# A pre-norm transformer block on one core: weight parts made by GpSimd in the middle head groups, the last shared block behind the expert tiles, and the first group's orders on ScalarE, VectorE and TensorE

## The chip, the cores and the metric

The kernel runs on one core of one Trainium2 chip. The metric is the device time of one execution in microseconds (us). TensorE is called PE below, VectorE DVE, ScalarE ACT, GpSimd POOL, and SP is SyncE, the queue from which nearly all DMAs are issued.

## The reference, cut to what matters

One block over 2048 rows of width 256, in f32: attention with 16 query heads in 4 groups (4 key and value heads) of width 16, then a feed-forward part with 8 experts, two of them for each row, and a shared expert.

```
x = x + attn(layernorm(x))                    # T = 2048, D = 256
  q, k, v = x @ ternary(w_qkv).T              # q, k: RMS norm, rotary, q * gain
  y = softmax(causal(q k^T / 4)) v            # 4 groups of 4 heads share k and v
  attn = rms_norm(y) @ ternary(w_proj).T
x = x + ffn(layernorm(x))
  scores = sigmoid(x @ w_router); top 2 of 8, weights normalised
  ffn = sum_e combine[:, e] * (silu(x @ w1[e]) * (x @ w3[e])) @ w2[e]     # F = 176
      + (silu(x @ ws1) * (x @ ws3)) @ ws2                                 # FS = 352
```

## The kernel before, in words

**Numbers as two parts.** An f32 operand of a matmul is held as a high part (rounded to fp32r) and a low part (what is left), and products are sums over parts. So each feed-forward weight must be split once: a copy that rounds (high) and a subtraction (low). The weights go through in 19 `PIECES`: 2 of the shared expert's up weights, 1 of its down weights, 8 of the experts' up weights (128x704), 8 of their down weights (88x512).

**Stages.** (1) Layernorm, projection, rotary for the first group. (2) Attention, one head group `g` after another. A group is 40 units `u`, pairs of a 512-column block `j` of queries and a 128-row block `kt` of keys: for each, PE makes scores (`scores`, L1528) two units ahead, ACT takes the exponential (`exps`, L772), and PE multiplies by the values (`times_values`, L1548). The units on the diagonal, u = 0 to 3, 8 to 11, 20 to 23 and 36 to 39, are masked by POOL in between (`mask`, L608): the product of such a unit waits for its mask. (3) The shared expert over four 512-row blocks `j` in three slices each, 12 steps `n` of `up(n)` and `down(n)` (L1666, L1681, L1686), with the last attention and routing steps between. POOL sends the rows, sorted by expert, to DRAM (`send_rows`, L649). (4) 39 expert tiles of 128 rows (L1720, L1738), each result scattered to DRAM by POOL (L710). (5) The two expert results of each row are loaded (`yfin`, L525), added (L1423), and stored.

**What sets the order.** Each engine runs its own list, written out by hand, and waits on semaphores; nothing reorders it. Tables say after which unit PE does something besides: `FIRST_GROUP`, `MID_GROUP`, `LAST_GROUP`, and `AFTER` for stage 3. A "round" `(g, c)` turns 512 rows of q and k for group g (PE, L1489), DVE splits it (`take_round`: the high part L1036, the low part L1037, then `x_free`), and SP moves the three copies of each part into place (`move`, 9 DMAs of 64 KB; two more for the shifts with c = 0). Group g + 1's rounds are made in group g at u = 26 to 36. The first group's own rounds are made inside it, at u = 1, 8 and 16.

**SP's list before**: the moves of group 0; 3 DMAs that clear the buffer of sorted rows in DRAM (`clear_rows`, 1935 KB each); the moves for group 1; 6 more clears; the moves for group 2; 9 DMAs that write row numbers (`pad_ids`, 4-byte elements); the moves for the last group; and then, in the last group, the loads of the 19 pieces into a staging buffer with two places (L491 to L503), each waiting for the piece two before it. The high parts are cast by DVE (`high_piece`, L1128) up to piece 8 and by ACT (L825) behind, the low parts subtracted by POOL (`low_piece`, L615) and, for the last four, DVE (L1287). All of these stand between other work in the lists of the last group and stage 3.

Of the kernel before, what the change touches and what calls it, by code (L numbers as in the profile page):

```python
# [56 lines left out]
Q_PARTS, K_PARTS = (0, 1, 0), (0, 0, 1)  # L57
# [7 lines left out]
SHARED_PIECES, EARLY_PIECES, POOL_PIECES = KD + 1, 9, 15  # L65
PIECE_COLS = 3 * D
NST = 2
RES_AFTER = {4: 1, 7: 2, 8: 3}
# [8 lines left out]
    1: [("round", 0, 1)], 4: [("out", 0, 0)], 8: [("round", 0, 2)], 12: [("out", 0, 1)], 16: [("round", 0, 3)],  # L77
# [8 lines left out]
    30: [("step", 6, 1)], 31: [("step", 2, 2)], 32: [("step", 3, 2)], 34: [("step", 7, 1)], 37: [("step", 4, 2)],  # L86
# [57 lines left out]
def build(nc, x, w_qkv, w_proj, q_gain, w_router, w1, w2, w3, ws1, ws2, ws3, rope_cos, rope_sin, out):  # L144
# [3 lines left out]
    with ExitStack() as ctx:  # L148
# [90 lines left out]
        wk_c = sb("wk_c", [P, NT, HS, HD], F32, prep)  # L239
        part1 = sb("part1", [P, QKV * D // P], BF16, prep)  # L240
# [40 lines left out]
        ld_stage = [sem(f"ld_stage{i}") for i in range(NST)]  # L281
# [22 lines left out]
        ones_ready = sem("ones_ready")  # L304
        ld_qk = [sem(f"ld_qk{c}") for c in range(NC)]
# [9 lines left out]
        piece_hi = sem("piece_hi")  # L315
        piece_done = sem("piece_done")
# [18 lines left out]
        hid_lo_ready = sem("hid_lo_ready")  # L335
# [21 lines left out]
        rows_d = nc.dram_tensor("rows_by_expert", (ROWS, ROW), F32, kind="Internal").ap()  # L357
        pair_d = nc.dram_tensor("pair_out", (2 * T + ROWS, D), F32, kind="Internal").ap()
# [28 lines left out]
        def piece_parts(n):  # L387

            buf = stage[:, n % NST, :]
            kind, *at = PIECES[n]  # L390
            if kind == "shared":
                k, = at
                return [(buf[:, 0:2 * FS].rearrange("p (w f) -> p w f", w=2), ws_hi[:, k], ws_lo[:, k])]
            if kind == "shared down":
                spans = [(P, 0, SH - 1), (shared_rows(SH - 1), SH - 1, SH)]
                return [(buf[0:r, a * D:b * D].rearrange("p (m d) -> p m d", d=D), ws2_hi[0:r, a:b, :],
                         ws2_lo[0:r, a:b, :]) for r, a, b in spans]
            if kind == "up":
                w, k, half = at
                es, fs = slice(half * E // 2, (half + 1) * E // 2), slice(w * F, (w + 1) * F)  # L400
                return [(buf[:, 0:E // 2 * F].rearrange("p (e f) -> p e f", f=F), w13_hi[:, k, es, fs],
                         w13_lo[:, k, es, fs])]
            h, pair = at
            es = slice(2 * pair, 2 * pair + 2)
            return [(buf[0:FH, 0:2 * D].rearrange("p (e d) -> p e d", d=D), w2_parts[0:FH, h, es, 0, :], w2_parts[0:FH, h, es, 1, :])]

        loads_of = {"shared": 2, "shared down": SH, "up": 1, "down": 1}

        def staged(n):

            return 16 * sum(loads_of[p[0]] for p in PIECES[n % NST:n + 1:NST])

# [4 lines left out]
        def _(sp):  # L417
# [19 lines left out]
            def move(g, c):  # L437
# [3 lines left out]
                sp.wait_ge(x_free, round_use(g, c))  # L441
                cs = slice(c * CH, (c + 1) * CH)
                for hf in range(2):
                    for n, part in enumerate(Q_PARTS):
                        sp.dma_start(qk_f[n:P:4, (g + 1) % 2, hf, cs],  # L445
                                     qT_f[2 * HD * hf:2 * HD * (hf + 1), part, cs]).then_inc(ld_qk[c], 16)
                if g > 0 or c >= K_BY_ACT:
                    move_k(sp, g, c, ld_qk[c])
# [7 lines left out]

# [11 lines left out]
            for c in range(NC):  # L468
                move(2, c)
# [1336 lines left out]
```

## Time and profile before

| | us |
|---|---|
| three runs | 583.75, 587.46, 588.2 (median 587.46) |
| the profiled execution | 586.47, its span 584.7, mean granted TensorE clock 0.91 |
| busy: PE, ACT, DVE, POOL | 474.4, 362.2, 314.9, 171.1 |

The span is shorter than the execution by 1.8 us, which lie around the first and last instruction. Busy time is read against the span; matmuls overlap, so a PE that is busy all the time may still wait a little in each unit. The granted clock is a share of 2.4 GHz. A wait is put down to the semaphore that came last.

### The profile page before, as it was taken

What the parts mean: (1) busy time and instruction counts of PE and PEld (TensorE: products, weight loads), DVE (VectorE), ACT (ScalarE), POOL (GpSimd) and SP (SyncE); (2) the same over time, 40 slices, a digit from 0 to 9 for tenths busy, and PEclk for the clock granted to TensorE, in tenths of its full rate; (3) what the DMA queues carried; (4) which work ended last, traced back from release to release, by engine and by line L of the source; (5) the groups of instructions that cost most, each with busy time, mean ns of one, the idle gap of its engine ahead of it and who ended that gap; (6) DMA issues with size and microseconds to landing.
All of it is one profiled execution on the core that took longest, in us unless ns stands there. A gap on an engine that the chain in (4) does not pass through costs nothing.

```text
span 584.7 us, 9812 instructions
## 1 busy us (share of the span) xinstructions
PE 474.4 (81%) x3202; PEld 265.1 (45%) x3202; DVE 314.9 (54%) x886; ACT 362.2 (62%) x567; POOL 171.1 (29%) x222
## 2 busy tenths in 40 slices
PE   1693949898999999999398978848888789999930
PEld 1581313333333333333143523326767679888930
DVE  6963615843732148031266485445948657666626
ACT  4244839897999999999359566615252335555520
POOL 3711100002110111103242145045455814444430
PEclk9878869999999999999789888868988989999975
DMA  7111011974799649624421113211111424444349
GB/s 207 36 42 41 2 40 30 278 204 107 214 298 296 164 77 4 2 53 110 138 57 62 26 46 114 62 34 64 30 55 40 123 73 119 117 119 128 101 132 353
DMA packets 77526, 61.37 MB, mean 105 GB/s; under 512 B 26984, under 2 KB 70600, under 8 KB 77480
## 3 DMA queue, kind: packets, MB, share of 16 engines
q1 hardware_dynamic: 73784, 51.04, 37.5%
q0 software_dynamic: 3408, 9.34, 4.4%
q8 instruction: 27, 0.44, 0.3%
q10 hardware_dynamic: 288, 0.39, 0.3%
q14 instruction: 19, 0.16, 0.1%
HBM read 19.88 MB, written 29.34 MB: 84 GB/s over the span
## 4 chain that ended last, share of the span: by engine, by line
PE 44%; DVE 15%; issue 13%; SPq 8%; DMA 7%; ACT 6%; POOL 5%; another core or an unknown queue 1%; ACTq 0%; POOLq 0%; DVEq 0%
PE ps L1548 14%; PE ps L1528 10%; PE ps L1720 6%; ACT prob L772 5%; SPq L445 4%; PE ps L1738 3%; POOL rows_by_expert L649 2%; PE ps L1468 2%; SPq L366 2%; PE ps L1557 1%; DMA qk<-qT 1%; PE ps L1711 1%; DMA yfin<-pair_out 1%; PE ps L1742 1%; PE ps L1489 1%
## 5 line engine op out<-in xcount | busy, mean ns | idle before, releaser
L772 ACT ACTIVATE prob<-ps 128x1024 f32<-128x1024 f32 (+3 forms) x320 | 260.1, 922 | 76.1 <-PE ps L1528 69.1
L1548 PE MATMUL ps<-prob,v_sb 128*32 128x512 f32 (+3 forms) x1280 | 156.8, 564 | 17.8 <-DVE o_sb L1048 9.0
L1528 PE MATMUL ps<-qk 64*128 64x512 f32 (+3 forms) x640 | 122.5, 448 | 24.1 <-DMA qk<-qT 15.3
L608 POOL TENSOR_SCALAR_AFFINE_SELECT prob<-prob 128x512 f32<-128x512 f32 x64 | 41.6, 652 | 233.7 <-ACT prob L772 232.8
L1528 PEld LDWEIGHTS ps<-qk 64*128 64x128 f32 x640 | 54.5, 194 | 118.2 <-ACT prob L772 82.2
L1548 PEld LDWEIGHTS ps<-prob,v_sb 128*32 128x32 f32 x1280 | 25.9, 110 | 65.1 <-issue 34.7
L710 POOL DMA_INDIRECT pair_out<-yo,xg x39 | 37.5, 963 | 56.1 <-DVE yo L1404 55.8
L1048 DVE COPY o_sb<-ps 128x512 f32<-128x512 f32 x16 | 11.0, 690 | 67.7 <-PE ps L1548 67.2
L1666 PE MATMUL ps<-x2T,ws_hi 128*128 128x512 f32 (+1 forms) x96 | 33.0, 428 | 5.4 <-DVE hid L1273 5.4
L649 POOL DMA_INDIRECT rows_by_expert<-xs,slots x32 | 31.2, 976 | 14.2 <-issue 8.6
L1036 DVE CAST qT<-ps 96x512 fp32r<-96x512 f32 x16 | 11.0, 686 | 38.6 <-PE ps L1489 38.6
L1738 PE MATMUL ps<-w_parts,ht_hi 88*128 x78 | 27.8, 437 | 1.4 <-issue 1.2
L856 ACT ACTIVATE sil<-ps 128x176 f32<-128x176 f32 x39 | 12.4, 318 | 25.5 <-PE ps L1720 25.5
L1391 DVE SCALAR_TENSOR_TENSOR hid<-sil,xg,ps 128x176 f32<-128x176 f32 x39 | 15.5, 397 | 18.1 <-ACT sil L856 17.6
L867 ACT COPY yl<-ps 128x256 f32<-128x256 f32 x39 | 14.5, 373 | 14.6 <-PE ps L1742 9.9
L1404 DVE TENSOR_TENSOR yo<-ps,yl 128x256 f32<-128x256 f32 x39 | 16.6, 425 | 11.6 <-ACT yl L867 10.6
L678 POOL TENSOR_TENSOR hid_lo<-hid,hid_hi 128x512 fp32r<-128x512 f32 (+1 forms) x12 | 15.5, 1299 | 24.5 <-ACT hid_hi L819 24.4
L1666 PEld LDWEIGHTS ps<-x2T,ws_hi 128*128 128x128 f32 (+1 forms) x96 | 17.6, 193 | 10.8 <-DVE hid L1273 6.3
L1054 DVE RECIPROCAL rec<-ps 128x16 f32<-128x16 f32 x16 | 4.1, 258 | 33.7 <-PE ps L1557 33.6
L615 POOL TENSOR_TENSOR w_lo<-stage,w_hi 128x704 fp32r<-128x704 f32 x8 | 13.5, 1692 | 28.6 <-DVE w_hi L1128 28.6
L1720 PE MATMUL ps<-w_hi,xt_hi 128*128 x78 | 19.9, 338 | 0.7 <-DVE xt_lo L1385 0.6
L1666 PE MATMUL ps<-x2T,ws_lo 128*128 128x512 f32 (+1 forms) x48 | 20.4, 426 | 0.0
(203 smaller groups left out, 781.2 us busy)
## 6 DMA issues: line engine op xcount, KB each, us to landing
rows_by_expert<-pads SPq DMA_DIRECT2D x9, 1935.0 KB, 20.4
qk<-qT SPq DMA_DIRECT2D x138, 64.0 KB, 2.1
xg<-rows_by_expert SPq DMA_DIRECT2D x39, 129.0 KB
yfin<-pair_out SPq DMA_DIRECT2D x8, 512.0 KB, 7.1
stage<-in_w SPq DMA_DIRECT2D x8, 352.0 KB
x_sb<-in_x SPq DMA_DIRECT2D x4, 512.0 KB, 6.8
qk<-shT SPq DMA_DIRECT2D x8, 256.0 KB, 4.8
res<-in_x SPq DMA_DIRECT2D x4, 512.0 KB, 4.1
```

The lines of the kernel that those rows point to most:

```text
L445: sp.dma_start(qk_f[n:P:4, (g + 1) % 2, hf, cs], qT_f[2 * HD * hf:2 * HD * (hf + 1), part, cs]).then_inc(ld_qk[c], 16)
L608: nc.gpsimd.affine_select(out=t, in_=t, compare_op=ALU.is_ge, fill=0.0, base=0, pattern=[[0, HPG], [1, P]], channel_multiplier=-1).then_in ...
L649: nc.gpsimd.indirect_dma_start(out=rows_d, out_offset=bass.IndirectOffsetOnAxis(ap=slots[:, j % 2, w, t:t + 1], axis=0), in_=xs_of[j][:, w ...
L678: nc.gpsimd.tensor_tensor(hid_lo[0:r, n % 2, :], hid[0:r, n % 2, :], hid_hi[0:r, n % 2, :].bitcast(F32), ALU.subtract).then_inc(hid_lo_rea ...
L710: nc.gpsimd.indirect_dma_start(out=pair_d, out_offset=bass.IndirectOffsetOnAxis(ap=xg[:, i % NXG, ID:ID + 1].bitcast(I32), axis=0), in_=yo ...
L772: nc.scalar.activation(prob[:, u % NPB, 2 * hf:2 * hf + 2, c0:CH], ps[:, b:b + 2, c0:CH], ACT.Exp, scale=SCALE).then_inc(exp_done, 1)
L1404: V.tensor_tensor(yo[:, i % NYO, :], ps[:, 4 + i % 2, 0:D], yl[:, i % 2, :], ALU.add).then_inc(yo_ready, 1)
L1528: ins = M(ps[:, 2 * (n % NSB) + h, c0:CH], qk[rows, par, PAIRS, kt * P:(kt + 1) * P], qk[rows, par, hf, j * CH + c0:(j + 1) * CH], start=T ...
L1548: ins = M(ps[VW * h:VW * (h + 1), O_BANK, c0:CH], v_sb[:, kt, :], prob[:, u % NPB, h, c0:CH], start=(kt == 0), stop=(u == LAST_OF[j]), ski ...
L1666: ins = M(ps[0:r, 2 * w + n % 2, :], wt[:, k, w, m * P:m * P + r], a[j][:, k, :], start=(i == 0), stop=(i == 3 * KD - 1))
L1720: ins = M(ps[:, i % 2, 0:UP], a[:, i % 2, k, :], w[:, k, bass.ds(e, 1), :].rearrange("p e f -> p (e f)"), start=(n == 0), stop=(n == 3 * K ...
L1738: M(ps[:, 4 + i % 2, :], ht_hi[0:FH, i % 2, h, :], w2_parts[0:FH, h, bass.ds(e, 1), :, :].rearrange("p e c d -> p (e c d)"), start=(h == 0 ...
```

## The change: what it does

Eight edits, together.

1. **The pieces are split two groups earlier, by POOL alone, and through DRAM.** SP loads a raw piece into one of `NRAW` = 3 places (`load_raw`), POOL casts and subtracts it (`split_piece`), SP stores both parts to new DRAM tensors (`store_parts`), of which two pieces fit at a time (`NSPLIT` = 2). POOL does 1 piece behind the mask of u = 3, 3 behind u = 11 and 6 behind u = 23 in groups 1 and 2 (`SPLIT_AT`). In the last group SP loads the finished parts: `ws`, `ws2`, `w13` (2 DMAs), and `w2_parts` after the attention.
2. **SP's list**: 4 clears ahead of the moves for group 1, 3 behind, then the first raw loads, 2 clears, and the pieces between the moves for group 2 and for the last group. The 9 writes of row numbers stand between the pieces of group 2.
3. All piece work leaves DVE, ACT and POOL in the last group and stage 3.
4. In `take_round` DVE signals the high part by itself (`hi_taken`); SP and ACT issue the moves of high parts at once and those of low parts after `x_free`.
5. First group: the round of c = 1 moves from u = 1 to u = 0; ACT's moves for it from before unit 3 to before unit 4; DVE's norm is cut into squares and scaling, and the squares stand earlier.
6. Stage 3: steps 4 to 7 of block 3 stand earlier in `AFTER`; step (4, 2) moves from u = 37 to 39; POOL keeps the low hidden part of n = 0 to 3, DVE takes it from n = 4; the rows of blocks 2 and 3 are sent without anything in between; `choose`, `place` and `list_tiles` stand earlier on DVE.
7. `up(11)` and `down(9)` to `down(11)` go behind the 39 tiles.
8. DVE adds the results of blocks 0 and 1, then the last shared block, then blocks 2 and 3. `yfin` lies over `w13` instead of `x2T`.

```diff
-Q_PARTS, K_PARTS = (0, 1, 0), (0, 0, 1)
+Q_PARTS, K_PARTS = (HI, LO, HI), (HI, HI, LO)
-NST = 2
+NRAW, NSPLIT = 3, 2
 FIRST_GROUP = {
-    1: [("round", 0, 1)], 4: [("out", 0, 0)], ...
+    0: [("round", 0, 1)], 4: [("out", 0, 0)], ...
-    ... 34: [("step", 7, 1)], 37: [("step", 4, 2)],
+    ... 34: [("step", 7, 1)], 39: [("step", 4, 2)],
-LOW_PIECES = {3: range(0, 3), 11: range(3, 5), 23: range(5, EARLY_PIECES)}
+SPLIT_AT = {3: 1, 11: 3, 23: 6}
+LOW_ON_DVE = range(4, FLAT)
 def move(g, c):                                   # SP
-    sp.wait_ge(x_free, round_use(g, c))
+    for want, ready, at in ((HI, hi_taken, NC * g + c + 1), (LO, x_free, round_use(g, c))):
+        sp.wait_ge(ready, at)
...
+def load_raw(n):
+    if n >= NRAW:
+        sp.wait_ge(split_done, n - NRAW + 1)
+    for r, at, shape, src, _ in pieces_of(n):
+        sp.dma_start(... raw[0:r, n % NRAW, ...], src).then_inc(ld_raw[n % NRAW], 16)
+def store_parts(n):
+    sp.wait_ge(split_done, n + 1)
+    ... sp.dma_start(to[part], ... parts_f[0:r, n % NSPLIT, part, ...]).then_inc(st_parts[n % NSPLIT], 16)
+def next_piece(n):
+    if n + NRAW - 1 < len(PIECES):
+        load_raw(n + NRAW - 1)
+    store_parts(n)
-clear_rows(0, 3)
+clear_rows(0, 4)
 for c in range(NC):
     move(1, c)
-sp.wait_ge(s_ready, 2 * NU)
-clear_rows(3, blocks)
+clear_rows(4, 7)
+sp.wait_ge(s_ready, 2 * NU + 2 * (LAG + 1))
+for n in range(NRAW - 1):
+    load_raw(n)
+clear_rows(7, blocks)
+for n in range(4):
+    next_piece(n)
 for c in range(NC):
     move(2, c)
+    if c < NC - 1:
+        next_piece(4 + 2 * c)
+        next_piece(5 + 2 * c)
+for n in range(10, 14):
+    next_piece(n)
+    number_pads(n - 10)
 for c in range(NC):
     move(3, c)
+    for n in range(14 + 2 * c, min(16 + 2 * c, len(PIECES))):
+        next_piece(n)
+        number_pads(n - 10)
...
+def split_piece(n):                               # POOL
+    pool.wait_ge(ld_raw[n % NRAW], raw_loaded(n))
+    if n >= NSPLIT:
+        pool.wait_ge(st_parts[n % NSPLIT], parts_stored(n - NSPLIT))
+    for r, at, shape, _, _ in pieces_of(n):
+        nc.gpsimd.tensor_copy(hi, a).then_inc(split_step, 1)
+        pool.wait_ge(split_step, taken["n"])
+        ins = nc.gpsimd.tensor_tensor(lo, a, hi.bitcast(F32), ALU.subtract)
+    ins.then_inc(split_done, 1)
+for g in range(NKV - 1):
     for u in range(NU):
         if on_diagonal(u):
             mask(g, u)
+        for _ in range(SPLIT_AT.get(u, 0) if g > 0 else 0):
+            split_piece(n)
...
+if n == FLAT - 1:                                 # PE, up(n)
+    pe.wait_ge(hid2_ready, TILES)
+    pe.wait_ge(ht_lo_ready, TILES)
+if n == FLAT_FIRST:                               # PE, down(n)
+    pe.wait_ge(yo_ready, TILES)
...
+up(FLAT - 1)                                      # PE, behind the tiles
+for n in range(FLAT_FIRST, FLAT):
+    down(n)
```

**POOL, from the masks of the middle groups on.** `prob` is the tile that a mask cuts, `raw` a loaded piece, `parts` its two parts. Before, the groups 0 to 2 are one loop of 16 masks, and the first piece stands behind the first four masks of the last group:

```order
76 L608 AFFINE_SELECT prob<-prob 128x4x128
77 L618 REGISTER_ALU
78 L618 COMPARE_AND_BRANCH
79 L608 AFFINE_SELECT prob<-prob 128x4x128 x4
80 L615 TENSOR_TENSOR ws_lo<-stage,ws_hi 128x704 x2
```

With the change, the loop is written out; row 46 is the 16 masks of group 0 and the first 4 of group 1:

```order
46 L667 AFFINE_SELECT prob<-prob 128x4x128 [waits exp_done] x20
47 L678 CAST parts<-raw 128x352 [waits ld_raw0]
48 L681 TENSOR_TENSOR parts<-raw,parts 128x352 [waits split_step]
49 L678 CAST parts<-raw 128x352
50 L681 TENSOR_TENSOR parts<-raw,parts 128x352 [waits split_step]
51 L667 AFFINE_SELECT prob<-prob 128x4x128 [waits exp_done] x4
52 L678 CAST parts<-raw 128x352 [waits ld_raw1]
```

The masks of u = 8 to 11 of group 1 (row 51) now stand behind a cast that waits for a load.

**SP, around the clears.** L445 and L366 move `qT` (DVE's parts of q and k) into `qk`. Before:

```order
21 L366 DMA qk<-qT 32x512 x3
22 L445 DMA qk<-qT 32x512 x6
23 L366 DMA qk<-qT 32x512 x3
24 L454 DMA rows_by_expert<-pads 128x15x258 x6
25 L445 DMA qk<-qT 32x512 x6
```

With the change (L379 and L387 move `qT`, L494 loads a raw piece, L502 stores parts):

```order
34 L379 DMA qk<-qT 32x512 x2
35 L387 DMA qk<-qT 32x512
36 L486 DMA rows_by_expert<-pads 128x15x258 x3
37 L494 DMA raw<-in_ws 128x352 x4
38 L486 DMA rows_by_expert<-pads 128x15x258 x2
39 L494 DMA raw<-in_ws 128x256 x2
40 L494 DMA raw<-in_ws 96x256
41 L502 DMA ws_parts<-parts 128x352 x4
```

The first raw loads stand behind all moves for group 1 and behind three clears.

## Rows read from the trace of the kernel before

**Rows 1.** Stages: us busy (instructions) of each engine, granted clock, DMA share, GB/s.

```profile
...
137.10:206.00 68.90, 67.13 (x517) 22.96 (x514) 26.34 (x58) 64.50 (x81) 10.27 (x16) 1.00 0.82 222
...
274.70:392.90 118.20, 89.76 (x622) 38.28 (x622) 61.85 (x240) 69.03 (x91) 37.09 (x41) 0.84 0.23 68
392.90:473.00 80.10, 66.57 (x378) 55.02 (x374) 54.86 (x138) 31.57 (x50) 46.15 (x42) 0.94 0.20 64
...
561.00:585.00 24.00, 0.17 (x2) 0.00 (x0) 10.26 (x10) 0.37 (x1) 1.93 (x2) 0.52 0.82 279
...
```

**Rows 2.** PE's waits: line, releaser, us in total, times, longest.

```profile
...
PE ps L1528 <- DMA qk<-qT: 15.3, 3, 7.5
...
PE ps L1548 <- DVE o_sb L1048: 9.0, 1, 9.0
PE ps L1548 <- POOL prob L608: 8.5, 1, 8.5
...
PE ps L1686 <- POOL hid_lo L678: 3.1, 2, 1.8
...
```

**Rows 3.** POOL in time, first masks of three quarters: start, us, what, idle before.

```profile
...
150.88 0.64 POOL L608 TENSOR_SCALAR_AFFINE_SELECT prob<-prob 128x512 f32<-128x512 f32 x1 [9.94 <-ACT prob L772]
...
200.23 0.64 POOL L608 TENSOR_SCALAR_AFFINE_SELECT prob<-prob 128x512 f32<-128x512 f32 x1 [24.98 <-ACT prob L772]
...
269.03 0.64 POOL L608 TENSOR_SCALAR_AFFINE_SELECT prob<-prob 128x512 f32<-128x512 f32 x1 [24.90 <-ACT prob L772]
...
```

**Rows 4.** DVE in time: high part of the round (2, 0).

```profile
...
184.22 0.69 DVE L1036 CAST qT<-ps 96x512 fp32r<-96x512 f32 x1 [3.04 <-PE ps L1489]
...
```

**Rows 5.** SP's issues in time: start, us, line, what, how many.

```profile
...
102.87 8.49 SPq L454 DMA_DIRECT2D rows_by_expert<-pads  x3
...
150.74 30.19 SPq L454 DMA_DIRECT2D rows_by_expert<-pads  x6
...
214.09 22.27 SPq L472 DMA_DIRECT2D rows_by_expert<-pad_ids  x9
254.53 3.67 SPq L445 DMA_DIRECT2D qk<-qT  x6
...
261.51 6.54 SPq L445 DMA_DIRECT2D qk<-qT  x6
...
```

**Rows 6.** DMA rate while six clears are under way (columns of Rows 1).

```profile
...
150.70:185.60 34.90, 33.93 (x262) 11.16 (x254) 15.03 (x34) 33.19 (x43) 5.18 (x8) 1.00 1.07 292
...
```

**Rows 7.** DMA issues from 185 to 187 us: KB each, us to landing.

```profile
...
qk<-qT SPq DMA_DIRECT2D x1, 64.0 KB, 6.8
```

**Rows 8.** Chain of waits from 280 to 292 us: start, us, what.

```profile
...
285.61 3.31 DMA stage<-in_ws
...
```

**Rows 9.** POOL's groups by form: busy us, mean ns, idle before, releaser.

```profile
...
L615 POOL TENSOR_TENSOR w_lo<-stage,w_hi 128x704 fp32r<-128x704 f32 x8 | 13.5, 1692 | 28.6 <-DVE w_hi L1128 28.6
...
L635 POOL COPY xs<-xs 128x1024 f32<-128x1024 f32 x2 | 2.1, 1050 | 8.9 <-DVE xs L1191 8.9
...
```

**Rows 10.** First PE work after the wait for o_sb (columns of Rows 1).

```profile
...
290.00:296.00 6.00, 4.65 (x24) 1.62 (x24) 2.89 (x10) 0.90 (x1) 2.10 (x3) 0.53 0.45 120
...
```

**Rows 11.** DVE and PE in time around the second long stall.

```profile
...
383.63 1.38 DVE L1191 TENSOR_SCALAR xs<-y_sb,mv,sm 128x256 f32<-128x256 f32 x4
...
391.55 0.66 PE L1562 MATMUL ps<-ident,xs 128*128 128x128 f32 x4
...
```

**Rows 12.** PE in time from the last shared block to the tiles.

```profile
...
461.37 0.62 PE L1666 MATMUL ps<-x2T,ws_hi 128*96 128x512 f32 x2
...
464.15 0.28 PE L1681 MATMUL ps<-ws_hi,hid_hi 128*128 128x256 f32 x1
...
471.65 0.93 PE L1711 MATMUL ps<-ident,xg 128*128 128x128 f32 x4 [0.94 <-DMA xg<-rows_by_expert]
...
```

**Rows 13.** DVE in time: a step beside a POOL subtraction; a block taken.

```profile
...
408.67 1.63 DVE L911 SCALAR_TENSOR_TENSOR sm<-sm 128x4 f32<-128x4 f32 x1
...
427.74 1.22 DVE L1279 TENSOR_TENSOR y_sb<-ps,y_sb 128x1024 f32<-128x1024 f32 x1
...
```

More of the change, by code:

```diff
@@ L239, in build @@
         wk_c = sb("wk_c", [P, NT, HS, HD], F32, prep)
+        split = ExitStack()
+        raw = sb("raw", [P, NRAW, PIECE_COLS], F32, split)
+        parts = sb("parts", [P, NSPLIT, 2, PIECE_COLS], F32R, split)
+        split.close()
         part1 = sb("part1", [P, QKV * D // P], BF16, prep)
@@ L280, in build @@
         ld_small = sem("ld_small")
-        ld_stage = [sem(f"ld_stage{i}") for i in range(NST)]
+        ld_raw = [sem(f"ld_raw{i}") for i in range(NRAW)]
+        split_done = sem("split_done")
+        split_step = sem("split_step")
+        st_parts = [sem(f"st_parts{i}") for i in range(NSPLIT)]
+        ld_ws = sem("ld_ws")
+        ld_w13 = sem("ld_w13")
+        ld_w2 = sem("ld_w2")
         ld_res = sem("ld_res")
@@ new lines, in _ @@
+            sp.dma_start(ws[:].bitcast(F32), ws_d).then_inc(ld_ws, 16)
+            sp.dma_start(ws2[:].bitcast(F32)[:, :, 0:SH - 1], ws2_d[:, :, 0:SH - 1]).then_inc(ld_ws, 16)
+            last_rows = shared_rows(SH - 1)
+            sp.dma_start(ws2[0:last_rows].bitcast(F32)[:, :, SH - 1], ws2_d[0:last_rows, :, SH - 1]).then_inc(ld_ws, 16)
+            sp.wait_ge(x_free, step_use(3, 0))
+            sp.dma_start(res[:], x_t[:, TPC:2 * TPC, :]).then_inc(ld_res, 16)
+            for part in range(2):
+                sp.dma_start(w13[:, part].bitcast(F32), w13_d[:, part]).then_inc(ld_w13, 16)
@@ L511, in _ @@
+            for j in range(2, NC):
+                sp.wait_ge(x_free, step_use(3, j - 1))
+                sp.dma_start(res[:], x_t[:, j * TPC:(j + 1) * TPC, :]).then_inc(ld_res, 16)
+            sp.wait_ge(pv_done, NPB + NU * NKV)
+            sp.dma_start(w2_parts[0:FH].bitcast(F32), w2_d).then_inc(ld_w2, 16)
             sp.wait_ge(rows_ready, 1)
@@ L1418, in _, with finish @@
                     tile_out(i - 2)
-            for c in range(NC):
+            def finish(c):
                 dve.wait_ge(ld_fin[c], 32)
@@ L1697, in _ @@
             pe.wait_ge(exp_done, NSB + 2 * NU * NKV)
-            pe.wait_ge(piece_done, SHARED_PIECES)
-            for n in range(FLAT + 2):
-                if n < FLAT:
-                    up(n)
+            pe.wait_ge(ld_ws, 48)
+            for n in range(FLAT - 1):
+                up(n)
                 after((n, 0))
```

354 lines of the change are left out of this document (171 added, 183 removed).

## The prediction, made before the change was run

> **What bounds the kernel now.** I read the stages first, then PE's waits, then the other engines in time where PE waits. In a middle group PE is busy 67.13 of 68.90 us at full clock, ACT 64.50, while DVE has 26.34 and POOL 10.27 [rows 1]: attention is bound by PE, and POOL looks free. The last group takes 118.20 us with PE at 89.76 and the granted clock at 0.84; the shared stage 80.10 with PE 66.57, DVE 54.86 and POOL 46.15. PE's longest waits there are one of 9.0 us for DVE's `o_sb` and one of 8.5 for a POOL mask [rows 2]. In both groups POOL's idle time is long but in pieces: it ends with the masks, which come in fours at fixed times (u = 8 of group 1 after 9.94 us of idleness, u = 36 after 24.98 and, in group 2, 24.90) [rows 3]. A list is worked off in order, so the question is whether the pieces put before a mask are done when that mask is wanted. If not, PE stops, since it has no slack there.
>
> **The first group.** DVE's signal for the high part saves the low half's time ahead of the first moves (0.7 us, the length of the high cast [rows 4]) in three rounds, and the earlier c = 1 and the cut norm some 1.2 to 1.3 in two of them; these waits are part of the 15.3 us behind `qT`'s moves [rows 2]. I take 2.0 + 1.2 + 0.7 = 3.9, less 1 because a fourth clear now lies before group 1's moves: **-3** (0 to -4).
>
> **Stall 1, group 1, u = 8.** The mask of u = 8 stands behind piece 0. It was wanted at 150.9 [rows 3], now at 147.9. SP used to begin the clears at 150.74; now, 3 us and one cast's 0.7 earlier, at about 147. Three clears take SP 8.49 us to issue [rows 5], so the raw loads go out at 155.5. The clears' data then move at 292 GB/s [rows 6], and 1935 KB is 6.6 us, three 19.8. If the loads queue behind them, they start at about 168; a small move issued while the last clear was draining landed only after 6.8 us [rows 7]. A free load takes 3.31 [rows 8]; with 2.5 for this smaller one and 3 for the four operations of piece 0 (a subtraction twice as wide is 1.69, a copy of 1024 columns 1.05 [rows 9]) the mask comes at about 174: **+26**. If the loads don't queue it is 155.5 + 3.3 + 3 = 162 and +14; with full clears and a landing of 6.8, +30. I take 26, since rows 7 show a transfer held on that very queue. Of "DMA: Bandwidth & Descriptors" in the Trainium skill, the section on queues, rings and completion order says that each DMA engine takes one queue's descriptors in ring order; by that rule it is the 26, without it the 14. The held move agrees.
>
> **Stall 2, group 1, u = 36.** Six pieces (4 to 9) stand between u = 23 and this mask, and SP's list threads them through the moves of the rounds. Before, the high part of round (2, 0) was made at 184.9 [rows 4] and the mask was wanted 15.3 us later [rows 3]. SP needs 6.98 for the moves of a first round and 0.61 for an issue [rows 5]. Piece 9's load goes out behind the moves of c = 0, four issues or so per piece and the moves of c = 1: 6.98 + 2 x 1.8 + 5.6 + 1.8 + 0.6 = 18.5. Its landing (3.3) and split (2.4 to 2.7) end at 24.5 to 25.5: **+10**. Low end 7, if small issues take less than 0.61; high end 14, with a landing of 6.8.
>
> **Stall 3, group 2, u = 36.** The same with pieces up to 18: the load of piece 18 goes out at 18 to 19, its places come free when the parts of piece 16 are stored (1.2 and 3.3 more), its split adds 2: 25 where 15.25 is there: **+10**. But writes of row numbers stand between, and each took SP 2.5 us (22.27 for nine [rows 5]) against the 0.6 I count; so 6 to 16.
>
> **The clock.** After the wait for `o_sb` PE works at a clock of 0.53 for 4.65 busy us [rows 10], so a stall costs some 2 more: **+6** for three (3 to 7).
>
> **The last group.** DVE's casts and the loads before them are gone, so the 9.0 for `o_sb` [rows 2] go with 2 of clock: **-11** (-7 to -12). The second, 8.5 for a mask that stood behind pieces on POOL, doesn't go whole. Step (4, 2) follows it, and needs `scale_x2`, which DVE ended at 385.0; PE came to that step's transposes at 391.55 [rows 11]. It can now be there at about 386.5, with 1 of clock: **-6** (-3 to -10). Fewer DVE and POOL operations otherwise: **-2** (0 to -4).
>
> **The shared stage.** `up(11)` took PE 2.8 us (461.37 to 464.15), the three `down` 7.5 with 2.7 of waits, so 4.8 [rows 12]. Together some 7.5 leave the way to the tiles. The 3.1 for `hid_lo` [rows 2] go with it. DVE's routing steps are freed of POOL's subtractions beside them (one of 4 columns took 1.63 instead of the 0.16 of its like [rows 13]) and stand earlier: 3. **-13.5** (-7 to -18). The Trainium skill, in "SBUF — State Buffer" on who interferes with whom, says that VectorE and GpSimd share a port pair with an exclusive lock; the row of 1.63 agrees. By that rule the 38 casts and subtractions now slow DVE in the middle groups instead. DVE is busy 26.34 of 68.90 there [rows 1], which covers it unless it falls on a round.
>
> **The tail.** What went behind the tiles is PE's work in 24 us in which it has 0.17 and DMAs move 279 GB/s [rows 1]. Only DVE's addition of one more block, 1.22 us [rows 13], may show: **+1.3** (0 to +3).
>
> **The sum** is made against the profiled execution, 586.5: -3 + 26 + 10 + 10 + 6 - 11 - 6 - 2 - 13.5 + 1.3 = +17.8, so 604.3. The profiled execution is 1.0 below the median of the three runs (587.46), so **605**. With all the terms at their best it is 569, with all at their worst 636; these don't fall together, and 592 to 618 is the forecast's own range.
>
> **The rivals.**
>
> *The waits are short and the gains win nothing (0.20).* The loads don't queue behind the clears, and the other two stalls sit at their low ends: 14 + 7 + 6 with 5 of clock is 32, against 34.2 of net gains (the other terms): 584.3, with the median's 1.0 some 585, and 577 to 592 with the gains' bounds. For it: no row shows a load from DRAM behind a clear, only the small move. Against it: that move's 6.8 us.
>
> *The pieces fit into POOL's idle time (0.07), the other side.* The mechanism is piece work that is ready each time before the next mask. It decides at u = 8 of group 1: the raw piece must have landed by about 145, which is before SP's clears end by every row of SP here, unless clears issued into an empty queue cost SP almost nothing. Then the stalls and their clock fall away and the gains stay: 586.5 - 34.2 + 1.0 = **553**. It turns into slower once the stalls with their clock come to over 34 us.
>
> *The stalls are longer than summed (0.13).* In group 2 the nine writes of row numbers take SP 22.27 us wherever they stand, and the small transfers queued behind them land in 6.8 instead of 3.3. Then stall 3 is at 16 and stall 2 at 14, stall 1 at 30 with 1 more of clock: 605 + 4 + 4 + 6 + 1 = **620**, up to 636.
>
> *The change doesn't do what it says:* SP's list, written out, has the loads where the diff says, behind three clears, and POOL's masks of u = 8 behind piece 0. I give this nothing of its own.
>
> **How the numbers follow.** The forecast has 0.60. A change of 1% (581.6 and 593.3) is what a measurement here can tell. Faster: 0.07, and 0.08 of the first rival: 0.15. Within 1%: the other 0.12 of it and 0.02 of the forecast's low edge: 0.14. Slower: 0.71. The range that holds 8 in 10 takes in most of the first rival and half of the third: 580 to 622.
>
> **What would show it.** Three waits of PE for POOL's `prob`, about 26 us in 148 to 174, 10 in group 1 and 10 in group 2, each before a mask that started late because a cast on POOL waited for `raw`; group 1 at some 105 us instead of 68.9, the last group at 100 instead of 118, the shared stage near 67, the tail still near 25, with no DVE wait of 9.0. If POOL's casts find their pieces landed, or SP's clears take less than 3 us in all, I am wrong at once; if the stalls are there but the time isn't, the gains of the last two stages were larger than their rows. A group 2 without a stall would say that the writes of row numbers cost SP little.

## The result, and the profile after

| | before | changed |
|---|---|---|
| executions, us | 583.75, 587.46, 588.2, 588.58 | 622.69, 630.32, 632.83, 635.2 |
| median | 587.83 | 631.58 |
| profiled execution, its span | 586.47, 584.7 | 622.69, 620.9 |
| mean granted clock | 0.91 | 0.891 |

The change makes the kernel slower: ratio 1.0652, 95% interval 1.0587 to 1.0716. Executions that were disturbed are in no ratio: here 632.83 and 635.2 (at a clock of 0.875), later 619.0 in experiment 1, 1393.16 and 577.75 in experiment 6, and one of 670.41 of the kernel before. The profiled execution was the shortest of its four. 605 was forecast, with 580 to 622 as the range: the direction is right, the size is not.

The stages of the changed kernel, cut at the same places as in [rows 1] (columns: us of the stretch, busy us and instructions of each engine, granted clock, DMA share, GB/s). They are group 1, group 2, the last group, the shared stage and the tail:

```profile
...
134.20:250.90 116.70, 72.65 (x522) 24.31 (x518) 25.03 (x58) 64.42 (x81) 36.73 (x44) 0.78 0.77 216
250.90:341.30 90.40, 70.95 (x514) 23.63 (x514) 28.36 (x57) 64.71 (x81) 28.21 (x35) 0.89 0.41 82
341.30:437.30 96.00, 83.27 (x618) 35.51 (x618) 54.79 (x222) 68.47 (x90) 21.53 (x31) 0.95 0.35 126
437.30:509.80 72.50, 60.05 (x330) 49.96 (x330) 47.99 (x149) 25.11 (x39) 28.18 (x28) 0.91 0.34 93
...
596.30:620.90 24.60, 7.28 (x50) 6.26 (x48) 12.71 (x13) 1.59 (x3) 1.97 (x3) 0.74 0.79 272
...
```

Group 1 takes 116.7 us with PE busy 72.65, where it took 68.9 with 67.13. PE's waits over the whole execution (us in total, times, longest):

```profile
...
PE ps L1609 <- POOL prob L667: 57.9, 4, 25.9
PE ps L1589 <- DMA qk<-qT: 11.7, 3, 6.9
...
PE ps L1747 <- DVE y_sb L1346: 4.4, 2, 2.5
...
PE ps L1609 <- DVE o_sb L1113: 3.4, 2, 2.6
...
```

The wait for POOL's `prob` was 8.5 us once [rows 2]; now it is 57.9 in four, 57.6 of it in groups 1 and 2. A ledger from mark to mark in the two profiled executions (the marks are the first mask of a group, the mask of u = 39 of the last group, the first tile's transposes, the end of the span):

| stretch | before | changed | difference | forecast |
|---|---|---|---|---|
| to the first mask of group 1 | 137.1 | 134.2 | -2.9 | -3 |
| groups 1 and 2 | 137.6 | 207.1 | +69.5 | +52 |
| last group, to the mask of u = 39 | 116.3 | 94.2 | -22.1 | -19 |
| on to the first tile | 80.6 | 73.0 | -7.6 | -13.5 |
| tiles and tail | 113.0 | 112.4 | -0.6 | +1.3 |
| sum | 584.7 | 620.9 | +36.2 | +17.8 |

**Stall 1.** The chain of waits of the changed kernel around u = 8 of group 1 (start, us, what):

```profile
...
148.00 1.94 SPq L486
...
149.98 6.85 SPq L486
...
156.88 6.02 SPq L494
...
162.94 9.26 DMA raw<-in_ws
...
172.81 0.93 POOL parts L681
...
```

It runs as forecast: SP issues three clears, then the raw loads from 156.88 on, which itself takes it 6 us, and they land 9.26 us later; POOL's piece 0 ends before 175.1, where the mask starts. PE waited 25.9 us (26 were forecast).

**Stalls 2 and 3.** SP's queue in the changed kernel (start, us of issuing, line, what, how many; L379 and L387 are moves, L494 a raw load, L502 stores of parts):

```profile
...
147.38 9.46 SPq L486 DMA_DIRECT2D rows_by_expert<-pads  x3
156.88 8.49 SPq L494 DMA_DIRECT2D raw<-in_ws  x4
...
210.98 2.39 SPq L379 DMA_DIRECT2D qk<-qT  x4
...
217.97 1.91 SPq L494 DMA_DIRECT2D raw<-in_w  x1
219.92 1.98 SPq L502 DMA_DIRECT2D w_parts<-parts  x2
...
233.05 0.79 SPq L494 DMA_DIRECT2D raw<-in_w  x1
233.88 1.83 SPq L502 DMA_DIRECT2D w_parts<-parts  x2
...
```

From 198.9 to 210.98 SP does nothing: it waits for the round (2, 0). Behind that move stand the loads of pieces 6 and 7 and the stores of pieces 4 and 5. POOL in the same execution (start, us, what, idle before and what ended it):

```profile
...
134.21 0.64 POOL L667 TENSOR_SCALAR_AFFINE_SELECT prob<-prob 128x512 f32<-128x512 f32 x1 [4.63 <-ACT prob L825]
...
172.25 0.48 POOL L678 CAST parts<-raw 128x352 fp32r<-128x352 f32 x1 [33.22 <-DMA raw<-in_ws]
...
226.49 0.77 POOL L678 CAST parts<-raw 128x704 fp32r<-128x704 f32 x1 [20.25 <-DMA w_parts<-parts]
...
240.84 0.77 POOL L678 CAST parts<-raw 128x704 fp32r<-128x704 f32 x1 [0.78 <-DMA w_parts<-parts]
...
243.31 1.81 POOL L667 TENSOR_SCALAR_AFFINE_SELECT prob<-prob 128x512 f32<-128x512 f32 x3
...
268.53 0.61 POOL L678 CAST parts<-raw 88x512 fp32r<-88x512 f32 x1
269.23 1.28 POOL L681 TENSOR_TENSOR parts<-raw,parts 88x512 fp32r<-88x512 f32 x1
270.45 0.61 POOL L678 CAST parts<-raw 88x512 fp32r<-88x512 f32 x1
271.14 2.12 POOL L681 TENSOR_TENSOR parts<-raw,parts 88x512 fp32r<-88x512 f32 x1
...
```

Piece 6's cast starts at 226.49 after 20.25 us of idleness, piece 9's at 240.84, and only at 243.31 comes the mask of u = 36, which had 16.80 us of PE waiting behind it. The row of 172.25 is stall 1: POOL idle for 33.22 us, for a raw load.

**The clock after a stall** (columns as in the stages):

```profile
...
150.00:175.00 25.00, 0.00 (x0) 0.00 (x0) 3.33 (x10) 1.18 (x3) 2.59 (x4) 0.58 1.08 295
175.00:181.00 6.00, 5.19 (x28) 1.53 (x32) 0.00 (x0) 1.02 (x3) 3.75 (x7) 0.50 1.12 277
181.00:187.00 6.00, 5.59 (x48) 1.93 (x48) 1.87 (x7) 6.00 (x7) 1.54 (x3) 0.98 1.08 292
...
```

In the 6 us behind stall 1 PE was busy 5.19 at half the clock (1.2 GHz), so 2.6 us are lost there. In groups 1 and 2 PE is busy 9.7 us longer than before with the same work, behind four stalls (the fourth is below).

**The tail.** From the timeline, PE and DVE behind the tiles:

```profile
...
596.34 2.94 PE L1730 MATMUL ps<-x2T,ws 128*96 128x512 f32 x12
...
602.94 0.64 PE L1752 MATMUL ps<-ws,hid_lo 96*128 96x256 f32 x4
606.28 2.48 DVE L1475 TENSOR_TENSOR y_sb<-y_sb,yfin 128x1024 f32<-128x1024 f32 x2 [4.14 <-DMA yfin<-pair_out]
...
```

The shared work moved there is over at 603.6, before the first result of an expert lands for DVE at 606.28.

### The profile page after: what moved, and what is told of

It is laid out like the page before. It is cut to its first block, busy times and chain, and to the rows that moved or that the text cites. A ratio compares the mean times of both kernels' runs of the same rounds, so it can differ in the third digit from the quotient of the medians.

```text
span 620.9 us, 9852 instructions
## 1 busy us (share of the span) xinstructions
PE 476.0 (77%) x3202; PEld 263.3 (42%) x3202; DVE 303.0 (49%) x880; ACT 356.4 (57%) x557; POOL 182.6 (29%) x244
## 4 chain that ended last, share of the span: by engine, by line
PE 45%; DVE 19%; SPq 14%; issue 8%; DMA 7%; ACT 5%; POOL 1%; DVEq 0%; ACTq 0%; POOLq 0%
PE ps L1609 13%; PE ps L1589 8%; PE ps L1785 6%; SPq L379 6%; ACT prob L825 4%; PE ps L1804 3%; PE ps L1730 3%; SPq L494 2%; SPq L387 2%; PE ps L1529 2%; SPq L486 2%; PE ps L1645 1%; DMA raw<-in_ws 1%; PE ps L1618 1%; SPq L502 1%
## 5 line engine op out<-in xcount | busy, mean ns | idle before, releaser
L1609 PE MATMUL ps<-prob,v_sb 128*32 128x512 f32 (+3 forms) x1280 | 162.0, 581 | 61.3 <-POOL prob L667 57.9
L1113 DVE COPY o_sb<-ps 128x512 f32<-128x512 f32 x16 | 11.1, 691 | 134.3 <-PE ps L1609 133.9
L678 POOL CAST parts<-raw 128x704 fp32r<-128x704 f32 (+4 forms) x23 | 14.9, 649 | 98.7 <-DMA raw<-in_ws 33.2
L1730 PE MATMUL ps<-x2T,ws 128*128 128x512 f32 (+1 forms) x144 | 40.4, 434 | 0.9 <-DVE hid L1332 0.9
L1785 PE MATMUL ps<-w,xt_hi 128*128 x156 | 31.7, 325 | 1.7 <-DVE xt_lo L1436 1.7
L1730 PEld LDWEIGHTS ps<-x2T,ws 128*128 128x128 f32 (+1 forms) x144 | 28.1, 201 | 8.8 <-DVE hid L1332 1.4
L681 POOL TENSOR_TENSOR parts<-raw,parts 128x704 fp32r<-128x704 f32 (+4 forms) x23 | 30.7, 1334 | 1.9
L882 ACT ACTIVATE sil<-ps 128x512 f32<-128x512 f32 (+1 forms) x12 | 7.2, 596 | 32.5 <-PE ps L1730 25.4
L1785 PEld LDWEIGHTS ps<-w,xt_hi 128*128 128x128 f32 x156 | 24.5, 188 | 2.1 <-issue 2.1
L916 ACT COPY yl<-ps 128x256 f32<-128x256 f32 x39 | 14.5, 373 | 14.7 <-PE ps L1808 9.6
```

Of the source, the lines that this page charges most:

```text
L681: ins = nc.gpsimd.tensor_tensor(lo, a, hi.bitcast(F32), ALU.subtract)
L1609: ins = M(ps[VW * h:VW * (h + 1), O_BANK, c0:CH], v_sb[:, kt, :], prob[:, u % NPB, h, c0:CH], start=(kt == 0), stop=(u == LAST_OF[j]), ski ...
L1730: ins = M(ps[0:r, 2 * w + n % 2, :], wt[:, k, w, m * P:m * P + r], a[j][:, k, :], start=(i == 0), stop=(i == 3 * KD - 1))
L1785: ins = M(ps[:, i % 2, 0:UP], a[:, i % 2, k, :], w[:, k, bass.ds(e, 1), :].rearrange("p e f -> p (e f)"), start=(n == 0), stop=(n == 3 * K ...
```

## The experiments

All on one core. Every ratio is to runs of the kernel before on the same chip; absolute times come from different chips (the medians of the kernel before lie between 582.55 and 588.25), so small differences are read from the ratios. Waits and stretches are those of one profiled execution each. "Wait for POOL" is PE's wait for `prob`.

**1. The raw loads ahead of the clears.**

```diff
+sp.wait_ge(s_ready, ...); load_raw(0); load_raw(1)
 clear_rows(4, 7)
-sp.wait_ge(s_ready, ...); load_raw(0); load_raw(1)
+next_piece(0); next_piece(1)
 clear_rows(7, 9)
```

> The changed kernel with the raw loads of pieces 0 and 1 ahead of the three clears (the last two clears behind the stores of piece 1). Theory 'the first stall is the queue': a transfer on SP's queue moves behind what was issued before it. The loads go out at 147.4, land at about 152, piece 0 takes 2.8: PE's wait for POOL before the product of u = 8 falls from 25.9 us to 3 to 7, the waits of 16.8 and 15.0 stay, and the time falls by 20 to 24, to 600 in the profiled execution (changed kernel: 622.7). Rival 'POOL or the DMA engines are slow there whatever the order': the wait stays over 15 and the time over 612.

612.9 us, ratio 1.040 (1.032 to 1.048). The first wait fell from 25.9 to 2.9 us; the others were 22.7 in two (5 of them new, at u = 20 of group 1) and 15.2. The order of SP's list made stall 1. The time fell less than the 20 to 24: from a ratio of 1.065 to 1.040, some 15 us, and PE's waits for masks by 16.8 us in all. The profiled execution took 619.0, where 600 was expected.

**2. Piece 0 loaded from ScalarE's queue, the clears in front as they were.**

```diff
 exps(1, 8)                                      # ACT
+nc.scalar.dma_start(raw piece 0)                # two loads
-load_raw(0)                                     # SP, behind the clears
```

> The changed kernel with the four raw loads of piece 0 issued by ScalarE behind the exponentials of unit 8 of group 1 (about 149.5 us), while the three clears stay ahead on SP's queue and are being moved. Theory 'each queue is in order, and queues share the engines': the loads land 3 to 8 us after their issue, the wait falls from 25.9 us to 8 to 12, the time by 13 to 18. Rival 'the DMA engines work off everything in order of issue': the wait stays at 22 to 26 and the time within 5 of the changed kernel's.

(Piece 0 has two loads; the four that the text speaks of are those of pieces 0 and 1.) The clears on SP, the two loads on ScalarE's queue and POOL's first cast, in time:

```profile
...
148.31 9.73 SPq L486 DMA_DIRECT2D rows_by_expert<-pads  x3
...
148.53 1.19 ACTq L862 DMA_DIRECT2D raw<-in_ws  x2
...
155.95 0.48 POOL L678 CAST parts<-raw 128x352 fp32r<-128x352 f32 x1 [15.23 <-DMA raw<-in_ws]
...
```

The loads were issued 0.2 us after the first clear and POOL could cast 7.4 us after that. Only two of the three clears had been issued by then, so the short time alone would not tell a second queue from a shorter one. The trace does: the first clear landed 9.9 us after its issue, at about 158, and the second at about 164, both behind the loads. From 149 to 155 us SP's queue moved 1.56 MB of the clears and ScalarE's the 0.36 MB of the loads, side by side: a second queue overtakes. The wait fell to 7.9. So the theory of queues stands, but the time did not fall as expected (626.6 us, ratio 1.0675, 1.061 to 1.074): waits later in groups 1 and 2 rose from 31.8 to 44.1 us. The load of piece 1 was still behind the clears on SP's queue (issued from 158.08, cast at 171.37), and a new wait of 11.9 stood at u = 20.

**3. No pieces at all, with the shared block behind and ahead of the tiles.**

```diff
-load_raw(n + 2); store_parts(n)                 # SP
+both parts of piece n copied from the input, DRAM to DRAM
-split_piece(n)                                  # POOL
```

> The changed kernel without raw loads and without POOL's casts and subtractions: at the same places of SP's list the inputs are copied from DRAM to DRAM into both parts (so the low parts are wrong, and the bytes written stay about the same). Theory 'the three stalls are POOL's list': all three waits for masks are gone, groups 1 and 2 take 138 to 140 us together instead of 207, and the time is 550 to 556, that is 0.94 of the kernel before. Rival 'the piece transfers themselves hold up the rounds of q and k': waits of PE for the moves of qT appear in place of the masks' and the time stays over 565.

> As no_pieces, but with up(11) and down(9) to down(11) ahead of the 39 tiles again, as in the kernel before. Theory 'the work behind the tiles is hidden by the last transfers': 6 to 9 us slower than no_pieces, all of it before the first tile. Rival 'it is only moved': within 2 us of no_pieces, the stretch behind the last tile being shorter by as much as the stretch before the tiles is longer.

573.5 us (0.973, 0.967 to 0.979) and 577.2 (0.982, 0.976 to 0.988). Groups 1 and 2 took 139.5 us as expected. But the time missed the 550 to 556, because the last group took 110.5, not 94: PE waited 10.4 us for DVE, which waited for the residual's rows. That wait was new. From the mask of u = 39 to the end it was 186.2 and 192.4 us, 6.2 more with the shared block ahead. The whole difference is smaller than the 6 to 9 expected: the medians are 3.7 apart, and the last group of the second run was 3.1 us shorter, which that edit does not explain.

**4. All transfers, but POOL doesn't wait for them or work on them.**

```diff
-pool.wait_ge(ld_raw...); pool.wait_ge(st_parts...); cast; subtract
+pool.sem_inc(split_done, 1)                     # parts filled once with a constant
```

> The changed kernel with all its transfers, but POOL neither waits for them nor casts nor subtracts: it fills the parts once with a constant and only counts the pieces (so all feed-forward weights are that constant; the earlier no_pieces had an artefact of its own, a wait of 10.4 us for a residual load). Theory 'the whole loss is POOL's list holding masks back': groups 1 and 2 take 138 to 141 us together, the last group 93 to 96, the time 554 to 560. Rival 'transfers': over 565, with waits for moves of qT.

577.6 us, ratio 0.983 (0.978 to 0.988): neither theory. The waits for masks are gone, but two others stand among PE's waits:

```profile
...
PE ps L1587 <- DMA qk<-qT: 16.4, 5, 6.9
...
PE ps L1643 <- DVE y_sb L1234: 9.2, 1, 9.2
...
```

L1587 waits for moves of `qT` (16.4 in five; 4.0 of it in groups 1 and 2, with 1.2 more for a shift, 1.0 in the last group, and the rest in the first), and L1643 waits 9.2 us for DVE's residual. Groups 1 and 2 take 146.3 us instead of 139.5 and the last group 106.8 instead of 94. So without the stalls, and with this list of SP's, SP's queue is the next bound, about 7 us in the middle groups, and the residual's load another 9. In the changed kernel neither wait shows: there the stalls gave the queue time.

**5. Pieces ahead of the moves, and a third place for parts.** The first changes SP's order only:

```diff
-for n in range(4): next_piece(n)
+for n in range(6): next_piece(n)
 for c in range(4):
     move(2, c)
-    next_piece(4 + 2 * c), next_piece(5 + 2 * c)      # c < 3
+    next_piece(6 + 2 * c), next_piece(7 + 2 * c)      # c < 2; group 2 alike
```

> The changed kernel with the stores and loads that follow pieces 4 and 5 (14 and 15 in group 2) ahead of the moves of round (2, 0) ((3, 0)) in SP's list; the later pairs move up with them. Theory 'the second and third stall are SP's order': there SP waited idle from 198.9 to 211.0 us for a round while piece 6's load and piece 4's store stood behind it. The waits of 16.8 and 15.0 us fall to 0 to 6 each, the 25.9 stays, and the time falls by 22 to 34, profiled execution 589 to 600 (changed kernel: 622.7). Rival 'bytes and places': the 1056 KB that a piece loads and stores at about 290 GB/s and the wait for a place of parts set the pace, and both waits stay over 11.

600.4 us, ratio 1.021 (1.017 to 1.026). What is left of the wait for POOL from 182 us on:

```profile
...
PE ps L1609 <- POOL prob L667: 6.9, 2, 5.9
...
```

16.8 became 5.9 and 15.0 became 1.0, both as expected; the first wait was 23.1. The other gives POOL more room:

```diff
-NRAW, NSPLIT = 3, 2
+NRAW, NSPLIT = 3, 3
```

> The changed kernel with three places for finished parts instead of two, nothing else. Theory 'SP's order': piece 6's raw load is behind the moves of round (2, 0) whatever the places, so the waits of 16.8 and 15.0 fall by 1 to 5 each and the 25.9 not at all; time 3 to 9 less. Rival 'the round trip of the stores': POOL's casts waited 27 and 31 us in all for stores of parts, so with a third place the two waits fall to under 8 each, and the time by over 16.

622.9 us, ratio 1.058 (1.051 to 1.065): the waits were 23.4, 15.1 and 13.4 (25.9, 16.8 and 15.0 before), 5.8 less in all, where two executions of the changed kernel differ by 3.9 (experiment 7). Order decided it, not places or bytes.

**6. Three rearrangements that keep all the work.** The first:

```diff
-SPLIT_AT = {3: 1, 11: 3, 23: 6}
+SPLIT_AT = {3: 2, 11: 4, 23: 4}
 move(1, 0); move(1, 1)
+load_raw(0); load_raw(1)
 move(1, 2); move(1, 3)
-...
+clears one at a time behind pieces 1 and 3, three in group 2
+one piece behind the moves of each round
+number_pads(0 to 8) in a row behind the moves for the last group
```

> The changed kernel with all its work, in another order: the first two raw loads ahead of the moves of rounds (1, 2) and (1, 3), POOL's pieces 2, 4 and 4 behind the units 3, 11 and 23 instead of 1, 3 and 6, one clear at a time between the pieces and three clears in group 2, and one piece behind the moves of each round. By my reading (order alone made the stalls) the waits for masks are under 4 us each, groups 1 and 2 take 139 to 147 us instead of 207, and the time is 555 to 565, 0.95 to 0.96 of the kernel before. Rival 'there is no room on the DMA queue': clears, pieces and moves of group 1 come to over 60 us of transfer in 69, and a wait of 8 to 15 us is left: 568 to 580.

604.8 us, ratio 1.029 (1.021 to 1.036), outside both. The waits for POOL came down to 3.2, 11.1 and 0.9, but a wait of 19.2 us for DVE stood in the last group. DVE's row of the residual, and SP's rows before it:

```profile
...
338.25 0.88 DVE L1244 SCALAR_TENSOR_TENSOR y_sb<-ps,y_scale,res 128x256 f32<-128x256 f32 x2 [20.72 <-DMA res<-in_x]
...
```

```profile
...
309.44 18.63 SPq L512 DMA_DIRECT2D rows_by_expert<-pad_ids  x9
328.19 2.50 SPq L560 DMA_DIRECT2D res<-in_x  x1
...
```

The nine writes of row numbers, 7.5 KB each, took SP 18.63 us in a row, and the residual's load stood behind them. The second takes up both waits: the stores and loads behind pieces 4 to 7 ahead of the move of round (2, 0), the writes spread over group 2, and two clears between the rounds of group 0.

> The rearranged kernel, with its two remaining waits taken up: 2, 3 and 5 pieces in group 1 and 2, 4 and 3 in group 2, the stores behind pieces 4 to 7 ahead of the moves of round (2, 0), five clears in group 0 (two of them before the move of its last round), one in the middle of group 1, three in group 2, and the nine writes of row numbers spread over group 2 instead of in a row in front of the residual's load. In the rearranged kernel these were waits of 11.1 us for a mask and of 19.2 us for DVE's residual, whose load stood behind 18.6 us of such writes. Theory 'each wait is a place in SP's list': both are under 4 us, groups 1 and 2 take 139 to 147 us, the last group 93 to 99, the time is 556 to 572. Rival 'SP's queue has no room for all of it': the waits come back elsewhere (moves of qT, masks) with over 10 us in all, and the time is over 575.

572.6 us, ratio 0.982 (0.977 to 0.986): just outside the 556 to 572. The residual's wait was 2.9, all but one of the masks' waits under 1.3, and that one 14.3, in group 2, behind two clears; groups 1 and 2 took 155.8 us, not 139 to 147. The third moves those as well:

```diff
 move(0, 1)
+clear_rows(0, 1)
 move(0, 2)
-clear_rows(0, 2)
+clear_rows(1, 3)
 move(0, 3)
-clear_rows(2, 5)
+clear_rows(3, 6)
 ...                                             # one more in group 1
-clear_rows(6, 8)                                # ahead of piece 12's load
+SPLIT_AT of group 2: {3: 2, 11: 3, 23: 4}
```

> The second rearrangement with the clears spread once more: six in group 0 (one behind the moves of its second round, two behind the third, three behind the fourth), two in group 1, one in group 2 behind piece 11, and 2, 3 and 4 pieces in group 2. In the run before, two clears in front of the raw load of piece 12 left one wait of 14.3 us for the mask of u = 20 of group 2. If a wait is only what stands ahead in the queue, no wait for a mask is over 3 us, groups 1 and 2 take 139 to 143 us, and the time falls by 13 to 19, to 554 to 560 (0.95 to 0.96 of the kernel before). If the queue has no room left, 5 us or more of waiting come back at another mask or at the moves of qT, and the time is over 563.

> The same with up(11) and down(9) to down(11) ahead of the tiles. By the pair no_pieces and no_pieces_shared_first (573.5 and 577.2, the stretch from the mask of u = 39 to the end 6.2 us longer) this is 4 to 7 us slower than rearranged_3. If that difference was chance, they are within 2 us.

**563.5 us, ratio 0.968 (0.966 to 0.971)**: faster than both kernels, though above the 554 to 560. Its waits that are left, and its groups 1 and 2 and last group:

```profile
...
PE ps L1624 <- POOL prob L682: 7.4, 3, 6.0
...
PE ps L1660 <- DVE y_sb L1251: 3.1, 1, 3.1
...
```

```profile
...
131.90:279.60 147.70, 136.00 (x1028) 46.12 (x1026) 55.34 (x114) 128.94 (x161) 66.41 (x78) 0.98 0.69 187
279.60:375.50 95.90, 82.09 (x606) 36.86 (x610) 53.22 (x214) 68.21 (x90) 19.84 (x27) 0.95 0.43 136
...
```

6.0 of the 7.4 is one mask, that of u = 20 of group 2: POOL's last cast before it waited 6.99 us for a store of parts, and SP's issues ahead of that store, behind a clear, took 2.3 to 3.5 us each. Groups 1 and 2 take 147.7 us where 139 to 143 were expected. That, and a time over 563, is what the expectation gave as the signs of a queue without room; whether yet another order would remove them was not tried. With the shared block ahead of the tiles it is 572.6 (0.9815, 0.978 to 0.986), 9 us slower where 4 to 7 were expected. Of the 9.5 us between the two profiled executions, 5.1 lie between the mask of u = 39 and the end (186.0 and 191.0 us); 3.0 lie in the last group and 1.3 before group 1, which that edit does not touch, and their cause is open.

**7. The changed kernel again.**

> The changed kernel again, to see where its executions differ (622.7 to 635.2 us in four; the profiled one was the shortest). If the stalls set by transfers vary, the three waits for masks come to more than 57.7 us by about what the execution is longer than 622.7; if it is the clock, they stay within 2 us of that and the granted clock is lower.

621.6 us (620.08 and 623.21), ratio 1.067 (1.061 to 1.074); waits of 21.5, 17.5 and 14.7, in all 3.9 less than in the first profile, for a span 2.6 shorter. So the stalls vary by some us from one execution to the next. So do the other stretches: to the first mask of group 1 it is 137.1 us here and 134.2 in the first profile, groups 1 and 2 take 203.6 and 207.1, the last group 91.2 and 94.2, the rest 186.5 and 185.4. Differences of up to 3 us in one stretch are therefore not firm. Why other executions took 630 to 635 us stays open: neither of these two was among them.

## Why the prediction was wrong in size and right in mechanism

The sum was made for the profiled execution: +17.8 forecast, +36.2 measured. Of the missing 18.4 us, 11.8 are stalls 2 and 3, 5.9 the clock with a fourth stall, and 5.9 the shared stage; the last group gave 3.1 more than forecast and the stretch from the tiles on 1.9. Another 8.9 lie between this execution and the median, and no trace shows where.

**First group** (-3): -2.9. The waits for `qT`'s moves fell by 3.6 us (3.9 forecast), and the wait for the shifts, which stands behind the fourth clear, grew by 1.5 (1 forecast). That the sum fits so well is partly luck: in experiment 7 the same kernel reached the mark at 137.1, as the kernel before did.

**Stall 1** (+26): the mechanism is right. The measured 25.9 fits better than it repeats, since it was 21.5 in experiment 7. Experiment 1 shows that it is the order in SP's list, and experiment 2 that it is the queue: the same loads from another queue landed ahead of clears that had been issued before them. The page "DMA: Bandwidth & Descriptors" of the Trainium skill, on queues and rings, says both, order within a ring and turns between rings; here it was 7.4 us from issue to use (experiment 2) against 15.4 (156.88 to 172.25).

**Stalls 2 and 3** (+10 and +10, measured 16.8 and 15.0): this is the step that failed, 11.8 us of the sum: SP's issues were priced too low, and in stall 2 the last wait was left out. It took 1.8 us of issuing per piece (three issues at 0.61, though the text says four or so), 5.6 for the moves of c = 1, a landing of 3.3, and for piece 9 no wait for the store that frees its place. From the high part of round (2, 0) at 210.9, piece 9's load was issued 22.1 us later, not 18.5: the issues for two pieces took 6.5 us instead of 3.6, the moves 6.7 instead of 5.6. And its place came free with the store of piece 7, which SP issues behind that load (to 235.1) and which landed after 5.64 us, so the cast began at 240.84, 29.9 after the high part. With 2.5 for the split the mask comes at 32.4, where 24.5 to 25.5 was worked out. I had taken the store into account in stall 3 and left it out in stall 2. In stall 3 the whole miss is SP's time: the load of piece 18 was issued at 327.76, 23.9 us after the high part of round (3, 0) at 303.84 (18 to 19 forecast), and its cast came 4.7 later, as worked out (4.5). Experiment 5 shows that the order causes both: with the pieces ahead, 5.9 and 1.0 are left.

**The clock** (+6, measured with a new stall 11.9): two parts. Three stalls cost 7.1 in clock (14.2 us of PE's busy time behind them at 1.2 GHz). The rest is a fourth stall that was not in the sum: 2.6 of waiting and 2.9 of clock, of which 0.7 came back elsewhere. DVE's work on the next round in group 2 lay beside POOL's pieces; DVE's rows, and PE's behind them:

```profile
...
269.49 1.10 DVE L1061 TENSOR_TENSOR sm<-sm,gain 128x64 f32<-128x64 f32 x1 [0.25 <-DVE sm L963]
270.62 1.52 DVE L1062 TENSOR_TENSOR wk_b<-qkv,sm 128x1024 f32<-128x1024 f32 x1
272.06 1.48 DVE L1064 TENSOR_TENSOR wk_b<-qkv,sm 128x256 f32<-128x256 f32 x1
273.67 0.69 DVE L1113 COPY o_sb<-ps 128x512 f32<-128x512 f32 x1
```

```profile
...
274.41 1.93 PE L1609 MATMUL ps<-prob,v_sb 128*32 128x512 f32 x8 [2.62 <-DVE o_sb L1113]
...
```

In the kernel before, the same three operations took 0.22, 1.22 and 0.42 us; here 1.10, 1.52 and 1.48, each beside a POOL cast or subtraction, together 2.2 longer. `o_sb` came that much later, PE waited 2.62 and then ran at half the clock. Where POOL did no piece work (experiment 4) the longest wait for `o_sb` in those groups was 0.4. The prediction had weighed this rule of the page "SBUF — State Buffer" of the Trainium skill, a port pair that VectorE and GpSimd share under an exclusive lock, and set it at nothing, with DVE's 26 busy us of 69 as the cover: the share hid that DVE is late at one place. It missed that masks do the same on a small scale. In the kernel before, steps of 0.24 us in DVE's chain take 0.5 to 0.7 beside a mask:

```profile
...
221.17 0.64 POOL L608 TENSOR_SCALAR_AFFINE_SELECT prob<-prob 128x512 f32<-128x512 f32 x1 [0.77 <-ACT prob L772]
...
221.32 0.58 DVE L910 TENSOR_TENSOR sm<-sm 128x80 f32<-128x80 f32 x1
...
```

In group 1 of the changed kernel POOL stood still at that time, and the same step took 0.24:

```profile
...
150.13 0.24 DVE L961 TENSOR_TENSOR sm<-sm 128x80 f32<-128x80 f32 x1
...
```

**Last group** (-19): -22.1, for which the terms were -11, -6 and -2. But experiments 3 and 4 show that this gain needs the residual's load in time. With nearly the same list of SP's and without the stalls PE waited 9 to 11 us for it; in the changed kernel it was in time, behind stalls that had given the queue nearly 60 us.

**Shared stage** (-13.5, measured -7.6): too large by 6. The shared block is 5.1 to 6.2 of it by two pairs of runs, with some 3 us of doubt (7.5 forecast). The 3.1 for `hid_lo` went, but PE now waits 4.4 for `y_sb` at L1747. All waits of PE in this stage came to 13.1 us before and to 12.7 after: they changed names, and the 3 us for an unhindered DVE are not to be found.

**Tail** (+1.3): -0.6 for tiles and tail together; the added block's work on PE is over before the results that DVE waits for.

**The rivals.** The third, longer stalls (620), came nearest: its stalls of 14 and 16 were nearest to the 16.8 and 15.0, though not for its reason, the writes of row numbers, which took 0.4 to 0.6 us each between the pieces. The pieces nearly fit into POOL's idle time, as the second supposed, but not with this list of SP's: 563.5 in experiment 6 against the 553 that it gave. Two sums of the prediction are off without changing its forecast: its worst terms together give 640, not 636, and POOL has 46 casts and subtractions, not 38.

## What to carry to other kernels

A list that is worked off in order passes its waits on: before placing work "in idle time", follow what it waits for through every queue it shares, and count the last transfer it needs (here a store), not the first. When a stall is taken away, look at what was hidden in it: the three stalls cost some 65 us with their clock, and what took them away met another wait each time, for `qT`'s moves, the residual's load or a mask behind a clear. Where one DMA queue carries bulk clears, small urgent moves and a pipeline through DRAM, order it by deadline; here SP's order, with POOL's pieces spread to match, turned 1.065 into 0.968.

## What the runs showed of the hardware that I had not expected

- Nine DMAs of 7.5 KB in 4-byte elements, issued in a row, kept SP for 18.6 us, and the queue moved 10 GB/s in that time (3 to 4 from 313 us on) at a DMA share of 1.50; spread among other work they cost SP 0.4 to 0.6 us each in the changed kernel.
- Two loads on ScalarE's queue, issued among the first two of three clears of 1935 KB on SP's, were usable 7.4 us after issue and before either clear had landed; behind all three, on SP's queue, it was 15.4 us from the start of the issue to the cast, and the issue came 8.4 us later.
- A stall of 25.9 us and one of 2.6 us were both followed by PE work at 1.2 GHz, 5.5 us of busy time behind the one and 5.8 behind the other; behind the stall of 15.0 us it was only 3.2.
- Beside a POOL mask of 0.64 us, a DVE step of 0.24 us took 0.58; beside a POOL subtraction of 2.12 us, one of 0.42 took 1.48.
